# One transfer per column group in place of four for the adjacency matrix of a graph-attention kernel

## The reference

```python
h = relu(layernorm(x))
Wh = h @ W
f1, f2 = Wh @ a1, Wh @ a2
e = leaky_relu(f1[:, None] + f2[None, :], 0.2)
e = where(adj == 0, -inf, e)
out = x + softmax(e, axis=1) @ Wh
```

## Time and profile before

| what | before |
|---|---|
| median of 3 runs | 900.22 us |
| lowest and highest | 898.43 and 901.08 us |
| the profiled execution's own time | 899.85 us |
| its span, first to last instruction | 898.2 us |
| PE busy | 845.0 us (94%) |
| DVE busy | 769.9 us (86%) |
| POOL busy | 153.2 us (17%) |
| mean granted TensorE clock | 0.982 |
| adjacency transfers | 256 of 256 KB written, 8.8 us (median) from issue to landing |

### The profile page before, as it was taken

The page is one execution under the profiler, slowest core; times in us unless marked ns, Lnnn a source line. Parts: engine busy times, 40 slices in busy tenths (PEclk is TensorE's granted clock), DMA queues, the critical chain, the costliest instruction groups (busy, mean ns, idle before and its releaser), DMA issues.

```text
span 898.2 us, 22755 instructions
## 1 busy us (share of the span) xinstructions
PE 845.0 (94%) x9475; PEld 775.6 (86%) x9475; DVE 769.9 (86%) x1333; ACT 67.3 (7%) x158; POOL 153.2 (17%) x279
## 2 busy tenths in 40 slices
PE   2848969999999999999999999999999999999997
PEld 1737859999999999999999999999999999999996
DVE  6825968889898989899898989898898989898996
ACT  2635100000000000000000000000000000000000
POOL 1212341111111111011110111101111111111000
PEclk9968989999999999999999999999999999999999
DMA  7970079999999898989899998999898998989500
GB/s 228 102 73 1 1 69 108 124 107 124 86 111 88 96 90 92 102 83 107 82 104 91 102 86 92 95 92 107 81 105 83 110 87 94 93 94 104 48 13 16
DMA packets 44029, 80.16 MB, mean 89 GB/s; under 512 B 4960, under 2 KB 5088, under 8 KB 44000
## 3 DMA queue, kind: packets, MB, share of 16 engines
q0 software_dynamic: 36864, 67.13, 78.0%
q1 hardware_dynamic: 7136, 12.65, 4.0%
HBM read 276.89 MB, written 4.19 MB: 313 GB/s over the span
## 4 chain that ended last, share of the span: by engine, by line
PE 90%; DVE 5%; DMA 2%; issue 2%; ACT 1%; POOL 0%; ACTq 0%; POOLq 0%; DVEq 0%
PE acc L303 50%; PE acc L307 26%; PE stage L284 12%; DVE row L464 1%; DMA xm<-in_adj_dram 1%; DVE wh L491 1%; PE acc L259 1%; ACT row L417 1%; DMA xm<-in_x_dram 1%; DVE wt_ring L551 1%; PE stage L247 0%; ACT ht L403 0%; ACT wh L388 0%; ACT L396 0%; POOL tmp L216 0%
## 5 line engine op out<-in xcount | busy, mean ns | idle before, releaser
L551 DVE SCALAR_TENSOR_TENSOR wt_ring<-row,packed,stage 128x512 f32<-128x512 uint8 (+1 forms) x1024 | 695.2, 742 | 99.2 <-PE acc L307 79.8
L303 PE MATMUL acc<-ht,wt_ring 128*128 128x258 f16 x4096 | 716.8, 274 | 2.5 <-DVE wt_ring L551 2.5
L307 PE MATMUL acc<-ht,wt_ring 128*128 128x129 f16 x4096 | 697.1, 219 | 0.0
L303 PEld LDWEIGHTS acc<-ht,wt_ring 128*128 128x128 f16 x4096 | 396.5, 97 | 60.6 <-DVE wt_ring L551 2.9
L307 PEld LDWEIGHTS acc<-ht,wt_ring 128*128 128x128 f16 x4096 | 399.9, 98 | 4.1
L199 POOL DMA_DIRECT2D xm<-in_adj_dram x256 | 135.5, 530 | 625.8 <-PE stage L284 574.9
L284 PE MATMUL stage<-ident,xm 128*128 128x128 f32 x1024 | 154.6, 274 | 8.4 <-DMA xm<-in_adj_dram 8.4
L284 PEld LDWEIGHTS stage<-ident,xm 128*128 128x128 f32 x1024 | 108.4, 141 | 12.3 <-DMA xm<-in_adj_dram 8.6
L413 ACT ACTIVATE fin<-acc 128x258 f32<-128x258 f32 x64 | 24.7, 386 | 749.1 <-PE acc L303 749.1
L268 PE MATMUL acc<-ident,packed 128*128 128x128 f32 x64 | 11.2, 347 | 14.8 <-DVE packed L538 12.5
L216 POOL TENSOR_TENSOR tmp<-wh,vf 128x516 f32<-128x516 f32 x16 | 16.6, 1044 | 44.1 <-DVE ht L559 35.1
(11 more groups left out here) (59 smaller groups left out, 54.1 us busy)
## 6 DMA issues: line engine op xcount, KB each, us to landing
xm<-in_adj_dram POOLq DMA_DIRECT2D x256, 256.0 KB, 8.8
xm<-in_x_dram SPq DMA_DIRECT2D x4, 1024.0 KB, 8.3
xo<-in_x_dram SPq DMA_DIRECT2D x16, 256.0 KB, 7.8
out_dram<-xo SPq DMA_DIRECT2D x16, 256.0 KB, 2.1
wx<-in_L_gnn_W_dram SPq DMA_DIRECT2D x1, 64.0 KB, 7.4
a_sb<-in_L_gnn_a_dram SPq DMA_DIRECT2D x1, 1.0 KB, 7.1
```

The lines of the kernel that those rows point to most:

```text
L303: return nc.tensor.matmul(acc[:, r, 0:2 * E1], wtv[:, w, r, 1, :], pairv[:, t, :, 0:E1], start=st, stop=end)
L307: return nc.tensor.matmul(acc[:, r, 0:E1], wtv[:, w, r, 0, :], pairv[:, t, 0, 0:E1], start=False, stop=False)
L551: nc.vector.scalar_tensor_tensor(out=wt_ring[:, t % NW, :], in0=row[:, bass.ds(q * BANK, BANK)], scalar=packed[:, 0, t:t + 1], in1=marks[: ...
```

## The change

Slots 4c to 4c + 3 lie next to each other in `xm`, so the four row blocks of a column group become one transfer: the view of memory is now ordered partition, row block, column, and the destination is 4 x 2048 bytes per partition. There are 64 transfers of 1 MB written in place of 256 of 256 KB. In the prologue the one transfer waits for the last of the four parts of x that its slots held. The semaphore counts at the waits shrink by four. The bytes moved and the rows read are the same.

```diff
-        adj_dram = adj.rearrange("(q p s) (c k) -> q s c p k", p=P, s=PACK, k=CHUNK)
+        adj_dram = adj.rearrange("(q p s) (c k) -> q c p s k", p=P, s=PACK, k=CHUNK)
...
+        def mask_group(c):
+            return xm[:, c * PACK:(c + 1) * PACK, :].bitcast(U8)
+
...
-            def load(q, c, r):
-                nc.gpsimd.dma_start(mask8(c * PACK + r), adj_dram[q, r, c]).then_inc(adj_loaded[c], 16)
-
-            for n in range(GC):
-                pool.wait_ge(s["xn_ready"], n + 1)
-                load(0, n // PACK, n % PACK)
+            def load(q, c):
+                nc.gpsimd.dma_start(mask_group(c), adj_dram[q, c]).then_inc(adj_loaded[c], 16)
+
+            for c in range(NC):
+                pool.wait_ge(s["xn_ready"], (c + 1) * PACK)
+                load(0, c)
...
                         pool.wait_ge(s["transposed"], (q - 1) * UN + (c + 1) * KC)
-                        for r in range(PACK):
-                            load(q, c, r)
+                        load(q, c)
...
-                    pe.wait_ge(adj_loaded[c], q * PACK * 16 + PACK * 16)
+                    pe.wait_ge(adj_loaded[c], q * 16 + 16)
```

More of the change, by code:

```diff
@@ L226, in _ @@
                     for c in range(NC):
-                        for r in range(PACK):
-                            pool.wait_ge(s["g_shift"], (q - 1) * GC + c * PACK + r + 1)
-                            load(q, c, r)
+                        pool.wait_ge(s["g_shift"], (q - 1) * GC + (c + 1) * PACK)
+                        load(q, c)
         @block.tensor
@@ L616, in _ @@
                             part, scale, total, valid = (gm[:, r, k:k + 1] for k in (4, 5, 6, 7))
-                            dve.wait_ge(adj_loaded[c], q * PACK * 16 + PACK * 16)
+                            dve.wait_ge(adj_loaded[c], q * 16 + 16)
                             nc.vector.tensor_scalar(drop, mask8(n), 1.0, NEG, ALU.subtract, ALU.mult)
```

## The result

The changed kernel takes 903.15 us (median of 9 runs, 902.05 to 905.37); the kernel before, in the same comparison, 900.3 (9 runs, 898.43 to 902.32). The ratio is 1.0032, 95% interval 1.0022 to 1.0042: slower by 0.3%, 2.85 us between the medians. In a later comparison on another occasion the same kernel gave 1.0017 (1.0004 to 1.003). The forecast was 901.8, range 898.8 to 905.8.

The account below looks back on a forecast made before the run. PE was taken to bound the main loop, with POOL's prologue and the first loads of q = 1 also on the path. Terms 0.67 + 0.3 + 0.6 = +1.6 us took 900.22 to 901.8 us, range 898.8 to 905.8.

Parts of the forecast that it names:

- What bounds the kernel: PE sets the time from 136 us on; before that, POOL's last issue and configurations, then the first loads of q = 1.
- Issue time, E = 1.2: POOL's issue of one 512-row transfer: taken as 1.2 us, between 0.53 and 2.1, against 0.53 for 128 rows.
- Last load, +0.67, "one for one": Prologue: the last load's longer issue delays configurations, reduction, flag and products equally, +0.67 us (0 to +1.6).
- Traffic beside the second configuration, +0.3: Prologue: 0.7 to 1 us more traffic slows POOL's configuration ahead of the first product, +0.3 us (0 to +1).
- First load of q = 1, +0.6: PE's wait near 120 to 131.8 us: the large transfer's data come later, +0.6 us (-0.7 to +1.6).
- rival C: Large transfers are cheaper, 11.6 us from the issue at q = 1; total 896.9 to 898.4; chance 0.06.
- Clock, 0 with both ends kept: PE's half clock behind each pause: taken as 0, could save 1.5 us or cost 1.7 us.
- The sum: 0.67 + 0.3 + 0.6 = +1.6 us, giving 901.8 for the median: no difference that can be told.
- Its own signs of being wrong: Further PE waits for transfers, a row group above 50.1 us, or configurations other than 9.8 and 6.6 to 7 us.
- A: Rows are the whole issue cost, 2.1 us, paid at 46.85 and 118.3: 903.7 to 905.4, slower; chance 0.30.
- B: The issue is flat, 0.53 to 0.7 us, only traffic costs in the prologue: 899.8 to 900.8; chance 0.17.
- D: The new row order slows the transfers in the main loop; at 30% slower, +70 us; chance 0.04.

Follow-up runs that it names:

- m1: Kernel before with single transfers kept in the prologue and merged ones for q = 1 to 15; 900.41 us, ratio 1.0002.
- n1: Changed kernel with the prologue's fourth transfer issued after the fourth product instead of ahead of the first configuration; 895.23 us, ratio 0.9933.
- n2: Changed kernel with the first two transfers of q = 1 issued ahead of products 8 and 12; 892.71 us, ratio 0.9912.
- m3: Kernel before, single transfers, each prologue load waiting for its whole column group's part of x; 902.04 us, ratio 1.0022.
- o1: Kernel before plus one 2 MB copy of x issued by SP once the flag is there; 904.75 us, ratio 1.0041.
- m0_before: Kernel before, run again without an edit for a second profile; 900.78 us, ratio 1.0004.
- o2_after: Changed kernel, run again without an edit for a second profile and comparison; 902.71 us, ratio 1.0017.
- before: First profile of the unchanged kernel, single transfers; profiled execution 899.85 us, median of 9 runs 900.3 us.
- o4_before: Kernel before, run again without an edit for a third profile; no run time given, first product at 66.83 us.
- o3: 128 transfers of two row blocks each, in prologue and main loop, instead of merged fours; 901.59 us, ratio 1.0007.
- m2: Kernel before with merged transfers in the prologue alone, single ones for q = 1 to 15; 901.58 us, ratio 1.0011.
- after: First profile of the changed kernel, merged transfers throughout; profiled execution 904.8 us, median 903.15 us, ratio 1.0032.
- n3: Changed kernel with both the edit of n1 and that of n2; 886.54 us, ratio 0.9836.
- n4: Both moves of n3, but with 256 single transfers; 887.14 us, ratio 0.9851.

## Why the prediction was right, and where not

*What bounds the kernel:* right. The main loop takes 50.0 us per row group with 60 transfers as with 240, and m1 puts no cost on them. The path goes through POOL's configurations and through the first load of q = 1; n1 and n2 show that by what their removal gives.

*Issue time, E = 1.2:* too high; it is 0.74. The choice "by the rows" had the wrong split: four times the rows cost little. The Trainium skill (DMA: Bandwidth & Descriptors, Anatomy of one DMA) says that many descriptors can be emitted before the incremental cost shows; the 0.03 us for 256 more rows agree. The 0.2 us between the single and the merged form are not in it.

*Last load, +0.67, "one for one":* failed in its size. The issue's excess was 0.21, and on the mean of the four profiles of each kind in the table the last issue ends at 47.8 in both. As a rule it could be neither seen nor refuted: the configuration behind it takes 7.8 to 9.8 us with single transfers on time, so its own scatter covers the effect, that of m3 (8.0) included.

*Traffic beside the second configuration, +0.3:* the mechanism was right, and o1 shows it; the size was not. Two things were undersized. The engines are busy for 2.7 us of it in place of 0.9, on the same means, 1.8 more where 0.7 to 1 was said. And a microsecond of that costs about 0.6, not the 0.32 that the ratio of the two configurations gave. That ratio rested on one 9.8; with the 7.8 to 9.8 of the other profiles the first configuration is no measure for what traffic does to the second. The term is +1.4 (7.0 to 8.4 us).

*The first configuration, for which the sum had no term beyond the issue:* 8.9 us with single transfers, 9.9 with merged ones, +1.0. What makes it isn't shown (below).

*First load of q = 1, +0.6:* not there. The issue is short, and the ten profiles listed under the table overlap in what passes from the first load to PE's restart; the 0.3 gained in the first pair is scatter. The large transfer took 13.2 us at q = 1, not the 11.6 that rival C reckoned with, and 12.5 in the main loop, against 13.8 from the first of four issues; there PE has no use for it.

*Clock, 0 with both ends kept:* it was right to keep both ends. But half clock doesn't follow each of PE's pauses, as the prediction had it. Behind the 2.27 us pause ahead of the main loop it is missing in m0_before, m1 and o2_after, and there it is 49.9 to 50.0 us from the first product to the first load of q = 1; it is 51.7 to 52.8 in before, o4_before, o3, m2, m3, o1 and after. So the clock moves an execution by up to 2.8 us, as much as the difference between the medians, and with single as with merged transfers. In the first pair of profiles it cost some 1.5 us, 0.96 in the row transposes and most of 0.6 behind PE's wait. Whether the change makes the half clock more likely, these few profiles can't tell.

*The sum:* 901.8 against 903.15. The three terms of 0.67, 0.3 and 0.6 became 0.2 at most, 1.4 and about 0, and 1.0 came in that the sum hadn't; so 2.4 where 1.6 was said, beside measured differences of 2.85, 1.4 and 1.1. That the total came close was luck: one term was too small and two too large.

*Its own signs of being wrong:* one of them was met. The configurations took 10.9 and 7.8 us, where "other than 9.8 and 6.6 to 7" was to refute it. The sign was badly chosen, since m0_before, with nothing changed, has 8.1 and 7.3. The issue (0.74 for 0.9 to 1.5), the first product (69.17 for 67.5) and the first load of q = 1 (3.7 us later, not 1) were outside what was forecast too; PE's one wait of 8.1 us and the 50.0 us of a row group were as said.

*Rivals:* A needed E from 1.7 on and is out. Its side, slower by over 0.3%, was nevertheless met in the first comparison, by another mechanism. B was nearest in the issue (0.53 to 0.7) and at q = 1, and is out by the prologue. C is out at q = 1, D by the 50.0 us of a row group and by m1.

**What stays open.** The first configuration took 10.9, 10.5, 9.0 and 9.2 us with a merged prologue, and with a single one on time 9.8, 8.1, 8.4, 9.2 and, in o1, 7.8, all under full traffic. That leans the same way but overlaps, and no run here changed the traffic beside the first configuration alone. So of the 2.4 us at the first product 1.4 have a cause that is shown, and 1.0 have not. Why traffic lengthens a configuration isn't shown either. And of the two comparisons of the changed kernel one gives 0.3%, the other 0.2%: that it is slower is measured, by how much only roughly.

## What to carry to other kernels

Merging transfers saves issue time, and that is worth nothing where the issuing engine waits anyway; what it costs is the start of the first parts, which then wait for the last. Look at what else runs while the transfers drain. Bulk transfers beside a GpSimd configuration lengthened it here (to 11.6 us in o1): issue only what is needed early, put the rest behind the last configuration, and issue the first loads of the next round ahead of the work that stands before them in the queue (n3, 1.6%). And take more than one profile of a kernel before a difference of 1 us between two is explained: here the clock and the configurations each scatter by more.

## What was not expected of the hardware

A configuration of GpSimd, 6.6 to 7.4 us with next to no traffic beside it (n1, n3, n4), took 11.6 under a 2 MB copy that ran from SP's queue, so it is not a matter of POOL's own transfers. The Trainium skill (GPSIMD Engine Reference, Instruction dispatch) puts the load that the first call of a freshly loaded kernel pays at approximately 6 us; the shortest here took 6.6. Such a gap is met twice, ahead of the reduction and on the way back to the product. A transfer's issue from GpSimd hardly costs by its rows (0.03 us for 256 more, 0.71 to 0.74) and more by its form (0.53 for the single one). A pause of PE of the same 2.27 us was followed by half clock in some executions and not in others.
